# Triangular inversions of a gated delta rule in 64x64 diagonal blocks, six heads per bank

## What is computed

```
S = S * exp(g_t)
delta = (v_t - k_t S) * beta_t
S = S + outer(k_t, delta)
o_t = q_t S
```

## Time and profile before

| | |
|---|---|
| median of 3 runs | 3656.5 us (3638.27 to 3669.38) |
| the profiled execution's own time | 3645.3 us |
| its span | 3643.6 us |
| PE busy | 2895.5 us (79%) |
| PE weight load busy | 2107.6 us (58%) |
| DVE busy | 1944.4 us (53%) |
| ACT busy | 1620.8 us (44%) |
| POOL busy | 801.9 us (22%) |
| mean granted PE clock | 0.845 |

### The profile page before, as it was taken

One profiled execution on the slowest core, in us unless ns is written; L12 is line 12 of the kernel. 1 busy time (PEld: TensorE's weight loads), 2 busy tenths in 40 slices (PEclk: granted clock), 3 DMA queues, 4 the chain that ended last, 5 costly groups with the idle time before them and its releaser, 6 DMA issues.

```text
span 3643.6 us, 61480 instructions
## 1 busy us (share of the span) xinstructions
PE 2895.5 (79%) x21172; PEld 2107.6 (58%) x21204; DVE 1944.4 (53%) x4849; ACT 1620.8 (44%) x3769; POOL 801.9 (22%) x517
## 2 busy tenths in 40 slices
PE   1577987789787897879868799787987779877897
PEld 1345764467644775547745477455764457644675
DVE  3346643566445664466543765537653466435664
ACT  0246442554326543365433744237442474425543
POOL 0014310243103321034200522004310143102331
PEclk7688997899878997789978899788986889878998
DMA  3300012010110003001030000300003000120101
GB/s 94 73 4 14 13 23 64 4 15 14 36 52 3 14 12 83 5 3 19 8 83 5 9 12 8 84 4 12 12 16 73 4 14 13 24 63 4 15 14 39
DMA packets 228743, 96.33 MB, mean 26 GB/s; under 512 B 176418, under 2 KB 218540, under 8 KB 226068
## 3 DMA queue, kind: packets, MB, share of 16 engines
q1 hardware_dynamic: 224178, 89.89, 11.8%
q10 hardware_dynamic: 4224, 2.10, 0.2%
HBM read 70.74 MB, written 21.17 MB: 25 GB/s over the span
## 4 chain that ended last, share of the span: by engine, by line
PE 48%; issue 19%; ACT 16%; DVE 8%; DMA 4%; SPq 3%; POOL 2%; DVEq 0%; ACTq 0%; POOLq 0%
PE bank L793 3%; PE bank L541 3%; PE bank L855 3%; PE bank L826 3%; PE bank L773 3%; PE bank L777 2%; PE bank L775 2%; PE bank L795 2%; PE bank L717 2%; SPq L1739 2%; PE bank L787 2%; PE bank L594 2%; DMA vq<-qk_bounce 2%; PE bank L805 2%; ACT arena L1549 2%
## 5 line engine op out<-in xcount | busy, mean ns | idle before, releaser
L1659 POOL TENSOR_TENSOR arena<-upto,gk 128x1536 f32<-128x1536 f32 x32 | 88.1, 2754 | 1379.9 <-DVE beta L1140 1379.9
L1147 DVE SCALAR_TENSOR_TENSOR arena<-bank,conv,arena 128x510 f32<-128x510 f32 (+1 forms) x384 | 285.8, 747 | 73.1 <-ACT arena L1437 50.0
L499 PE MATMUL bank<-vq 72*128 72x128 bf16 (+3 forms) x512 | 185.9, 426 | 158.4 <-DMA vq<-qk_bounce 136.6
L1037 DVE TENSOR_REDUCE mx<-bank 128x1 f32<-128x128 f32 (+3 forms) x512 | 220.3, 486 | 146.0 <-PE bank L500 138.1
L1651 POOL TENSOR_TENSOR arena<-arena 128x511 f32<-128x511 f32 x192 | 243.6, 1271 | 223.2 <-DVE arena L1147 223.0
L665 PE MATMUL bank<-h_t,arena 128*128 128x512 f32 x384 | 226.0, 684 | 51.2 <-DVE arena L1147 51.1
L1524 ACT COPY u<-bank 32x128 f32<-32x128 f32 x192 | 49.6, 258 | 472.2 <-PE bank L787 471.1
L1400 ACT ACTIVATE arena<-bank 128x384 f32<-128x384 f32 (+1 forms) x384 | 174.0, 536 | 165.3 <-PE bank L527 165.3
L717 PE MATMUL bank<-vq 64*128 64x128 f32 x1536 | 168.1, 317 | 52.8 <-ACT arena L1511 36.5
L499 PEld LDWEIGHTS bank<-vq 72*128 72x128 bf16 x512 | 65.1, 128 | 231.0 <-issue 149.0
L717 PEld LDWEIGHTS bank<-vq 64*128 64x128 f32 x1536 | 146.4, 212 | 74.9 <-ACT arena L1511 38.4
(11 more groups left out here) (294 smaller groups left out, 6926.6 us busy)
## 6 DMA issues: line engine op xcount, KB each, us to landing
vq<-qk_bounce SPq DMA_DIRECT2D x162, 128.0 KB
arena<-w_bounce SPq DMA_DIRECT2D x16, 1024.0 KB, 14.9
qk_bounce<-arena SPq DMA_DIRECT2D x18, 384.0 KB, 2.5
arena<-in_L_attn_Wv_dram SPq DMA_DIRECT2D x8, 768.0 KB, 18.9
t<-t_bounce SPq DMA_DIRECT2D x256, 12.0 KB, 1.8
x<-t_bounce SPq DMA_DIRECT2D x256, 12.0 KB, 1.8
arena<-in_L_attn_Wq_dram SPq DMA_DIRECT2D x8, 384.0 KB, 13.4
arena<-in_L_attn_Wk_dram SPq DMA_DIRECT2D x8, 384.0 KB, 15.5
```

What stands on the lines that cost most here:

```text
L499: mm(ps[:, 0:e], q_stack[0:KS, h, t * P:e], k_stack[0:KS, h, 0:e], start=True, stop=False)
L1037: last = V.reduce_max(mx[:, h, t:t + 1], score_bank(n)[:, 0:(t + 1) * P], AX.X)
L1147: ins = V.scalar_tensor_tensor(a[:, k:T], ps[:, 0:T - k], conv[:, n, 3 - k:4 - k], a[:, k:T], ALU.mult, ALU.add)
```

## The change

The steps 0 to 5 only ever hold something in the two 64x64 diagonal blocks. `t16`, `x16`, `u32`, `ub` and `tw` now keep those alone, 64 columns per head, the first block in partitions 0 to 63 and the second in 64 to 127; `mask16d` is the mask in this form. With 64 columns a bank of PSUM holds LH = 6 heads, so there are NL = 2 groups instead of 3, in banks 0, 1 and 4, 5. Steps 0 to 2 make two 64x64 products per head, on partitions 0 to 63 and 64 to 127; steps 3 to 5 are in 32x32 tiles for all heads; steps 6 and 7 are 64x64 products. DVE evicts step 1 in two halves, since `xw` keeps its 128x128 form. The lower left of `xw` is no longer written, so the inverse product is made of two matmuls per head, 128x64 and 64x64 weights. Waits follow the new counts; in the fourth stage (c = 3) the wait for `wo_done` stands ahead of step 0 instead of step 1; the gate of the middle chunks waits once. PE increments a semaphore that nobody waits for, `lv_go`, ahead of each group in six of the steps. SP's DMAs scatter to the compact places, as many as before.

Cut: the counts in `IN_ROW`, names that only follow, and the removed body of PE's `levels`, which is printed above.

```diff
@@ -61,6 +61,8 @@
...
+    NL, LH = 2, 6
+    L_16, L_SB, L_PS = 3 * NL, 5 * NL, 8 * NL
@@ -159,19 +162,20 @@
...
-        dt, bm, ub, tw, xw = heads(dec_a), heads(bm_a), heads(ub_a), heads(t_a), heads(x_a)
+        dt, bm, xw = heads(dec_a), heads(bm_a), heads(x_a)
+        ub, tw = heads(ub_a[:, 0:HD * DK], DK), heads(t_a[:, 0:HD * DK], DK)
...
-        osq, ogt, og = rb, xw, tw
+        osq, ogt, og = rb, xw, heads(t_a)
...
-        t16 = sb("t16", [P, HD, P])
-        x16 = sb("x16", [P, HD, P])
-        u32 = sb("u32", [P, HD, P])
+        t16 = sb("t16", [P, HD, DK])
+        x16 = sb("x16", [P, HD, DK])
+        u32 = sb("u32", [P, HD, DK])
...
-        gate = tw
+        gate = og
@@ -323,7 +327,7 @@
...
-            return PS[s % 2 * 3 + g]
+            return PS[s % 2 * 4 + g]
@@ -751,56 +755,55 @@
                         pe.wait_ge(pt_ready, at(b, pt_ready, NG * (c + 2)))
                     else:
                         pe.wait_ge(o_ready, at(b, o_ready, NG * c))
+                        pe.wait_ge(wo_done, at(b, wo_done, c - 1))
                     for s in range(8):
-                        for g in range(NG):
-                            if s == 1 and g == 0 and c + 1 == NT:
-                                pe.wait_ge(wo_done, at(b, wo_done, c - 1))
+                        for g in range(NL):
                             if s == 1:
                                 pe.wait_ge(lv_16, at(b, lv_16, n16 + g + 1))
                             elif s == 3:
-                                pe.wait_ge(lv_16, at(b, lv_16, n16 + 2 * NG + g + 1))
+                                pe.wait_ge(lv_16, at(b, lv_16, n16 + 2 * NL + g + 1))
                             elif s == 4:
                                 pe.wait_ge(lv_sb, at(b, lv_sb, nsb + g + 1))
                             elif s == 6:
-                                pe.wait_ge(lv_sb, at(b, lv_sb, nsb + NG + g + 1))
+                                pe.wait_ge(lv_sb, at(b, lv_sb, nsb + NL + g + 1))
                             elif s == 7:
-                                pe.wait_ge(lv_sb, at(b, lv_sb, nsb + 3 * NG + g + 1))
+                                pe.wait_ge(lv_sb, at(b, lv_sb, nsb + 3 * NL + g + 1))
+                            if s != 2 and s != 5:
+                                pe.sem_inc(lv_go, 1)
                             ps = level_bank(s, g)
...
+                            for j in range(LH):
+                                h = LH * g + j
+                                o = j * DK
+                                if s == 6:
+                                    last = mm(ps[DK:P, o:o + DK], bms[c % 2][0:DK, h, DK:P], tw[0:DK, h, :], start=True, stop=True)
+                                    continue
+                                if s == 7:
+                                    last = mm(ps[0:DK, o:o + DK], u64[DK:P, h, :], xw[DK:P, h, DK:P], start=True, stop=True)
+                                    continue
+                                for q in (0, DK) if s != 4 else (0,):
+                                    r = slice(q, q + DK)
+                                    up, low = slice(q, q + 32), slice(q + 32, q + DK)
+                                    if s == 0:
+                                        out_at, lhs, rhs = ps[r, o:o + DK], bms[c % 2][r, h, r], t16[r, h, :]
+                                    elif s == 1:
+                                        out_at, lhs, rhs = ps[r, o:o + DK], ub[r, h, :], x16[r, h, :]
+                                    elif s == 2:
+                                        out_at, lhs, rhs = ps[r, o:o + DK], x16[r, h, :], ub[r, h, :]
+                                    elif s == 3:
+                                        out_at, lhs, rhs = ps[low, o:o + 32], bms[c % 2][up, h, low], tw[up, h, 0:32]
+                                    elif s == 4:
+                                        out_at, lhs, rhs = ps[low, o:o + 32], xw[low, h, low], u32[low, h, 0:32]
+                                    else:
+                                        out_at, lhs, rhs = ps[up, o + 32:o + DK], u32[low, h, 0:32], xw[low, h, low]
+                                    last = mm(out_at, lhs, rhs, start=True, stop=True)
                             last.then_inc(lv_ps, 1)
 
                 def gate_proj(c):
                     for g in range(NG):
                         if c + 1 == NT and g == 0:
                             pe.wait_ge(o_ready, at(b, o_ready, NG * NT))
-                        elif c + 1 < NT and g:
-                            pe.wait_ge(lv_sb, at(b, lv_sb, 5 * NG * (c + 1) + 4 * NG + g))
+                        elif c + 1 < NT and g == 2:
+                            pe.wait_ge(lv_sb, at(b, lv_sb, L_SB * (c + 1) + 4 * NL + 1))
                         ps = gate_banks(c)[g]
                         mm(ps[:, :], h_t[:, c * P:(c + 1) * P], wgate[:, g * 512:(g + 1) * 512], start=True, stop=True).then_inc(gt_ps, 1)
 
@@ -813,7 +816,7 @@
...
-                        pe.wait_ge(lv_sb, at(b, lv_sb, 5 * NG * (c + 1)))
+                        pe.wait_ge(lv_sb, at(b, lv_sb, L_SB * (c + 1)))
@@ -830,11 +833,12 @@
...
-                            pe.wait_ge(lv_sb, at(b, lv_sb, 5 * NG * (c + 1)))
+                            pe.wait_ge(lv_sb, at(b, lv_sb, L_SB * (c + 1)))
...
-                            last = mm(ps[:, j * P:(j + 1) * P], xw[:, h, :], rb[:, h, :], start=True, stop=True)
+                            mm(ps[DK:P, j * P:(j + 1) * P], xw[:, h, DK:P], rb[:, h, :], start=True, stop=True)
+                            last = mm(ps[0:DK, j * P:(j + 1) * P], xw[0:DK, h, 0:DK], rb[0:DK, h, :], start=True, stop=True)
@@ -1172,7 +1175,7 @@
...
-                            dve.wait_ge(lv_ps, at(b, lv_ps, 24 * (c - 2) + 21))
+                            dve.wait_ge(lv_ps, at(b, lv_ps, L_PS * (c - 2) + 7 * NL))
@@ -1199,17 +1202,16 @@
...
-                    n16 = 3 * NG * c
...
-                        for g in range(NG):
-                            hs = slice(GH * g, GH * (g + 1))
-                            dve.wait_ge(lv_ps, at(b, lv_ps, 24 * c + NG * s + g + 1))
-                            ps = level_bank(s, g)[:, :].rearrange("p (h t) -> p h t", h=GH)
+                        for g in range(NL):
+                            hs = slice(LH * g, LH * (g + 1))
+                            dve.wait_ge(lv_ps, at(b, lv_ps, L_PS * c + NL * s + g + 1))
+                            ps = level_bank(s, g)[:, 0:LH * DK].rearrange("p (h t) -> p h t", h=LH)
...
-                                ins = V.tensor_tensor(ub[:, hs, :], ps, mask16[:, :].unsqueeze(1).to_broadcast([P, GH, P]), ALU.mult)
+                                ins = V.tensor_tensor(ub[:, hs, :], ps, mask16d[:, :].unsqueeze(1).to_broadcast([P, LH, DK]), ALU.mult)
@@ -1217,7 +1219,8 @@
...
-                                ins = V.tensor_tensor(xw[:, hs, :], x16[:, hs, :], ps, ALU.subtract)
+                                V.tensor_tensor(xw[0:DK, hs, 0:DK], x16[0:DK, hs, :], ps[0:DK], ALU.subtract)
+                                ins = V.tensor_tensor(xw[DK:P, hs, DK:P], x16[DK:P, hs, :], ps[DK:P], ALU.subtract)
@@ -1513,25 +1516,23 @@
...
-                        for g in range(NG):
-                            hs = slice(GH * g, GH * (g + 1))
-                            act.wait_ge(lv_ps, at(b, lv_ps, 24 * c + NG * s + g + 1))
-                            ps = level_bank(s, g)
-                            full = ps[:, :].rearrange("p (h t) -> p h t", h=GH)
-                            part = ps[:, 0:GH * DK].rearrange("p (h t) -> p h t", h=GH)
+                        for g in range(NL):
+                            hs = slice(LH * g, LH * (g + 1))
+                            act.wait_ge(lv_ps, at(b, lv_ps, L_PS * c + NL * s + g + 1))
+                            ps = level_bank(s, g)[:, 0:LH * DK].rearrange("p (h t) -> p h t", h=LH)
...
-                                    ins = A.copy(u32[r, hs, q], full[r, :, q])
+                                    ins = A.copy(u32[r, hs, 0:32], ps[r, :, 0:32])
...
-                                ins = A.mul(tw[r, hs, q], full[r, :, q], -1.0)
+                                ins = A.mul(tw[r, hs, q], ps[r, :, q], -1.0)
...
-                                    ins = A.mul(xw[q, hs, r], full[q, :, r], -1.0)
+                                    ins = A.mul(xw[q, hs, r], ps[q, :, 32:DK], -1.0)
...
-                                ins = A.copy(u64[DK:P, hs, :], part[DK:P])
+                                ins = A.copy(u64[DK:P, hs, :], ps[DK:P])
...
-                                ins = A.mul(xw[0:DK, hs, DK:P], part[0:DK], -1.0)
+                                ins = A.mul(xw[0:DK, hs, DK:P], ps[0:DK], -1.0)
@@ -1629,7 +1630,9 @@
...
-            keep(mask16[:, :].rearrange("p (q i) -> p q i", q=4), [[32, 4], [0, 32]], 31, -1, 0.0).then_inc(masks_made, 1)
+            then(keep(mask16[:, :].rearrange("p (q i) -> p q i", q=4), [[32, 4], [0, 32]], 31, -1, 0.0))
```

(15 more changed lines are left out.)

32 lines of the change are left out of this document (2 added, 30 removed).

## The result

The changed kernel takes 3780.3 us, the median of six runs (3773.2 to 3794.1), against 3657.3 before: 1.034 times as long, interval 1.031 to 1.038. The profiled execution took 3794.1 us, with a span of 3792.4 and a mean granted clock of 0.805 (before: a span of 3643.6 and 0.845). It is the slowest of the six, and the profiled one of before lies 11 us under its median, so the two traces differ by 149 us where the medians differ by 123. I had said slower, 3700 and at most 3770.

What follows compares the result with a forecast made beforehand. Bound: mostly PE's program order, PE 100% busy in the inversion stages. Per sample -21.0 (stages, net) + 21.2 (inverse product) + 6 (clock) = +6.2; times 8, +50 on 3656.5: 3706, said 3700; range 3475 to 3770.

Steps and rivals of the forecast that it cites:

- the step that decides it: Inverse product L837: its two weight shapes, differing in rows, do not run side by side; 8.8 us instead of 2.7.
- the clock: Scans: drained pairs of L837 bring the lower clock; 1.5 us on each scan, 0 to 4, 6 us per sample.
- The size of the product: Inverse product L837, drained: 24 x 0.365 = 8.8 us; L855 begins 5.3 us later, 21.2 us a sample lost.
- the other side: Rival: the two shapes of L837 run side by side; 3497 us, between 3460 and 3560; chance 0.33.
- Stages: Four inversion stages of a sample: 80.1 us together become 14 each, 24.1 us saved, bounds 18 and 32.
- the increments of `lv_go`: 12 instructions on PE's queue per stage, between 0 and 0.25 us each; taken as 0, standing after waits.
- Step (a): Stage 1: DVE waits for POOL (L1687), so at most 3.5 us can be had where 5.7 were counted: -2.2.
- The wait for `wo_done`: Stage 3, ahead of step 0: needs DVE's L1287 and L1289 of the projection; 0.9 us a sample lost.
- The second: Rival: L837 drained, but the clock holds; about -30 us, from 3600 to 3660; chance 0.18.
- the result is near 3640: Sign to look for: granted clock over the scans stays at 1.0 and L837 is at 9 us.
- the third rival: 64x64 passes of steps 0 to 2 don't overlap, or `lv_go` breaks PE's queue; about 3790, undrained 3590; chance 0.07.

Runs made afterwards that it cites:

- the second and the third experiment: Inverse product split by columns alone, on the changed kernel with xw in its own zeroed buffer: 3565.3 us; the split alone on the kernel before: 3829.8 us.
- POOL's order: POOL's squares for the rms moved ahead of its mask and scaling: on the changed kernel 3717.8 us, 1.015; on the kernel before 3668.6 us, 1.001.

## Why the prediction was right and wrong

The sign was right, and the step that decides it held: the two shapes of the inverse product do not run side by side. The step that failed is the clock. I put 1.5 us on every scan because drained pairs would pull the clock down; the pairs did so in none of 32 scans, though they stood in the way of its return once it had fallen, and the loss came at one scan of four, 9.4 us, out of a wait of PE that I had not put into the sum. Besides, I took the stages before from one sample that was longer than the others, and put at nothing the gaps behind the stages and the way to the next sample.

The size of the product was right as well. A pair was put at 0.365 us and measured 0.361, the product at 8.8 and measured 8.7, the delay of the output at 5.3 a scan and measured 4.9 to 5.7, 21.2 us a sample against 20.4. What the trace of before could not decide, whether it matters that they share no cells, is decided by the second and the third experiment: it does not matter. The chance of 0.33 for the other side was too high for what the rows said, that no change of shape had ever gone free. The Trainium skill (TensorEngine Tiling, Key Properties) says that a change of tiling mode drains TensorE, and the 0.36 us a pair against 0.11 with one shape agree with it. The Trainium skill (TensorEngine Tiling, Gotcha 1: PSUM Pressure) also says that different row tiles can't use one PSUM bank at the same time, and there the trace disagrees: the 64x64 passes of two row tiles into one bank stood 30 ns apart, near the 29 that the prediction took for tiles that overlap and half of the 58 that it took for one tile alone.

The size of the whole was wrong, +43 us for +123; per sample the sum had +6.2, the medians have +15.4 and the two traces +18.4. Term by term, per sample, by the traces:

- Stages: 24.1 us forecast, 20.4 measured. The pitch and the 5.6 us to step 3 (5.7) were right, and so nearly was the length, forecast at 14: without the wait behind the fourth, the four stages are 13.4, 14.5, 14.3 and 14.8 us long, 1.0 us a sample more than forecast. What was too large is the 80.1 us that I took off from, the stages of one sample; over all eight they are 77.6. The lower clock set in later than step 3, mostly 7 to 10 us into the stage where step 3 begins at 5.7. I took nothing for the increments of `lv_go`, because they stand after waits; just there a second one cost 0.15 us. If the first ones cost as much, which no run shows, they are some 3 us a sample, and something else in the stages was put too high by 2.
- Step (a), the bound of the second stage by POOL and DVE: right in its place, since DVE waited 3.48 us for POOL and its 3.5 us of spare time were gone. But I booked it only as a gain that can't be had. It was a new wait of PE, 1.5 us, and that wait is where the clock falls: 2.5 us in the keys and queries and 17.41 - 10.55 = 6.9 in the product, 9.4 us. POOL's order changed and the wait gone, both came back in every sample.
- The clock: 6 us forecast, for a reason that fell. I had drained pairs pull the clock down in every scan, from L575/L576. They did in none: with POOL's order changed, all 32 products run at 1.00, and the three other scans did so without it. L575/L576 come behind several waits of PE, which I passed over when I read the pairs for the cause; no run separates the two there. The timeline of PE in the kernel before:

```profile
1073.61 0.33 PE L570 MATMUL bank<-ident,arena 128*128 128x128 f32 x1 [0.29 <-DVE arena L1055]
1074.32 0.33 PE L570 MATMUL bank<-ident,arena 128*128 128x128 f32 x1 [0.38 <-DVE arena L1055]
1075.32 0.49 PE L575 MATMUL bank<-wproj,arena 128*128 128x128 f32 x2 [0.68 <-ACT arena L1408]
```

- The gaps behind the stages: nothing forecast, 3.1 us measured; their mean clock is 0.61 to 0.84 where it was 0.72 to 0.92. I had no term for that. That the lower clock comes from the stage ahead, which gives PE less to do up to its end, is my reading; no run tests it.
- The wait for `wo_done`: 0.9 forecast, 0.91 in the trace. Undoing it took 0.98 us off that place and put 1.26 on stage 3, at a lower clock. So its length alone, by which I priced it, says too little.
- From one sample to the next the last part is 4.1 us longer, 33 us of the whole, and I had nothing for it. 2.0 of them are PE's wait for the transfer of the stacks, ahead of the first scores of the next sample: 15.2 us on average against 13.2. It runs from 8.4 to 17.9 us over the samples of the changed kernel and from 9.3 to 19.1 before, and it averages 16.2 in the kernel before with POOL's new order. So 2 us are no more than the same work varies by. 1.6 more lie ahead of that wait, at a mean clock of 0.80 against 0.85. No experiment was made on it, and whether the change has a part in it stays open.

Two of the rivals bear on this. The second, drained with the clock held, was to give 3600 to 3660 us, and I had written that with the scans at 1.0 and the product at 9 us the result is near 3640. The changed kernel with POOL's order is that case, and it took 3717.8: what the clock does in the scans is not all that the sum lacked. And the third rival's 3790 lies near the 3780 measured by luck, since the 64x64 passes did overlap and an increment cost at most 0.15 us where it had 0.25.

## What to carry to other kernels

Count the changes of shape of the weights, not the matmuls: with weights of two shapes in turn, each pair of passes paid 0.36 us where pairs of one shape on alternating columns paid 0.11. Giving the weights a buffer of their own and zeroing the part that the smaller shape left out, so that one matmul does for both, was worth 219 us. Where a PE stage gets shorter, look for what else stands in the other engines' programs at that place and was covered by it: here the place of a 2.7 us piece in POOL's order, harmless before (1.001), cost 62 us after. And where a wait of PE falls not long after a stretch of small matmuls, price it at the work that follows at the lower clock and not at its own length. Last, take a term of a sum from all repetitions of a stretch and not from one: here that was 2.5 us a sample.

## What the runs showed of the hardware that I hadn't expected

- 48 passes with 64 columns of weights on alternating columns start two at a time, 0.11 us apart, so they cost what 24 of 128 columns do; on one tile alone passes with 128 columns streamed stand 0.117 apart, whether the weights are 128x64 or 64x64.
- A second semaphore increment in PE's program, for which nobody waits, cost 0.15 us at a group that PE waits for and nothing behind passes still to be done.
- A wait of 1.5 us in the second scan, with a stage at 0.75 not long before it, was followed by the lower clock, while 8.7 us of drained pairs without such a wait left it at 1.00. With POOL's new order the same scan had the lower clock behind waits of 0.89 to 0.95 us (three samples of the sixteen of two kernels) and kept the full one behind 0.44 to 0.84. In the kernel before, where the stage ahead had a mean clock of 0.91, it kept the full one behind 0.91.
- One matmul of 0.9 us in a wait raised the mean clock of the stage around it from 0.82 to 0.91 in stage 0 and not at all in stage 1.
